# Mask phase of a two-layer cross-attention kernel: row sums scaled at another place, casts and the first turn in a new order

## The reference, cut to what matters

```python
xq = layer_norm(x, qn_w, qn_b)
ctx = layer_norm(context, cn_w, cn_b)
q = xq @ q_w;  k, v = halves of ctx @ kv_w          # 16 heads of 32
attn = einsum('bnhd,bmhd->bhnm', q, k) * scale
attn = where(xa_mask, -max, attn)
attn = softmax(attn, axis=-1)
out = einsum('bhnm,bmhd->bnhd', attn, v) @ proj_w + proj_b
x = x + out
```

## Time and profile before

| What | us |
|---|---|
| median of three runs | 2664.84 (2664.46 to 2666.05) |
| the profiled execution's own time | 2662.04 |
| its span in the profile | 2660.3 |
| busy TensorE | 2592.9 (97%) |
| busy VectorE | 1940.7 (73%) |
| busy ScalarE | 1559.0 (59%) |
| busy GpSimd | 922.3 (35%) |
| mean granted clock of TensorE | 0.995 of full |

### The profile page before, as it was taken

The page is one execution under the profiler, slowest core; times in us unless marked ns, Lnnn a source line. Parts: engine busy times, 40 slices in busy tenths (PEclk is TensorE's granted clock), DMA queues, the critical chain, the costliest instruction groups (busy, mean ns, idle before and its releaser), DMA issues.

```text
span 2660.3 us, 67274 instructions
## 1 busy us (share of the span) xinstructions
PE 2592.9 (97%) x23144; PEld 2230.5 (84%) x23144; DVE 1940.7 (73%) x5443; ACT 1559.0 (59%) x4742; POOL 922.3 (35%) x1098
## 2 busy tenths in 40 slices
PE   6999999998999999999999999999999999999997
PEld 5788888887888888888888888888788888888886
DVE  6888888887534443444378888887788888888877
ACT  6787777876211111111267777777676776767764
POOL 4766676662111001100113333333442434424331
PEclk9999999999999999999999999999999999999999
DMA  5766667674210211022021111112321322212210
GB/s 165 184 165 168 168 170 189 165 189 132 72 59 32 63 47 47 32 63 87 25 96 48 47 47 47 47 47 80 100 80 63 98 68 71 87 63 95 71 48 25
DMA packets 313622, 236.12 MB, mean 89 GB/s; under 512 B 150736, under 2 KB 240848, under 8 KB 312656
## 3 DMA queue, kind: packets, MB, share of 16 engines
q1 hardware_dynamic: 313552, 235.22, 30.9%
HBM read 137.65 MB, written 63.96 MB: 76 GB/s over the span
## 4 chain that ended last, share of the span: by engine, by line
PE 77%; DVE 10%; ACT 7%; issue 4%; POOL 0%; DMA 0%; DVEq 0%; ACTq 0%; POOLq 0%; SPq 0%
PE cross_work L181 17%; PE mlp_acc L3297 13%; PE mlp_f L3279 13%; PE causal_work L181 10%; PE cross_scores L2294 3%; PE mask_work L181 3%; ACT mask_prob_even L965 2%; ACT mask_prob L965 2%; PE cross_scores L2271 2%; PE cross_attended L2324 2%; PE causal_scores L2294 2%; PE causal_scores L2271 2%; DVE mask_scores L1552 2%; PE causal_attended L2324 2%; DVE mask_stats L1465 1%
## 5 line engine op out<-in xcount | busy, mean ns | idle before, releaser
L3072 ACT ACTIVATE mlp_h<-mlp_f,mlp_b1col 128x512 f32<-128x512 f32 x128 | 88.3, 690 | 525.9 <-PE mlp_f L3279 525.9
L3279 PE MATMUL mlp_f<-mlp_xT_hi,mlp_w 128*128 128x512 f32 x1024 | 335.7, 390 | 0.9 <-DVE mlp_xT_lo L3165 0.9
L3179 DVE CAST mlp_hT_hi<-mlp_h 128x512 fp32r<-128x512 f32 x128 | 58.2, 454 | 369.9 <-ACT mlp_h L3072 369.7
L3297 PE MATMUL mlp_acc<-mlp_w,mlp_hT_hi 128*128 128x512 f32 x1024 | 315.5, 389 | 0.0
L965 ACT ACTIVATE cross_prob<-cross_scores,cross_low 128x256 f32<-128x256 f32 x512 | 237.1, 490 | 63.4 <-DVE cross_low L1546 63.4
L965 ACT ACTIVATE causal_prob<-causal_scores,causal_low 128x128 f32<-128x128 f32 (+1 forms) x512 | 210.1, 436 | 93.7 <-DVE causal_low L1552 93.6
L3279 PEld LDWEIGHTS mlp_f<-mlp_xT_hi,mlp_w 128*128 128x128 f32 x1024 | 192.3, 188 | 41.3 <-DVE mlp_xT_lo L3165 1.3
L3297 PEld LDWEIGHTS mlp_acc<-mlp_w,mlp_hT_hi 128*128 128x128 f32 x1024 | 192.3, 188 | 39.8
L181 PE MATMUL causal_work<-causal_xT_hi,causal_w 128*128 128x256 f32 x1008 | 217.1, 294 | 0.3 <-DVE causal_qk_parts L1500 0.3
L1552 DVE CUSTOM_DVE_ANT_0 mask_scores<-mask_scores,mask_mask 128x256 f32<-128x256 f32 x512 | 200.5, 456 | 22.1 <-PE mask_scores L2271 13.6
L736 POOL TENSOR_SCALAR causal_q<-all_own_head,causal_qk_parts 128x128 fp32r<-128x128 f32 x128 | 60.1, 481 | 406.2 <-DVE causal_qk_parts L1500 395.9
(11 more groups left out here) (369 smaller groups left out, 8093.4 us busy)
## 6 DMA issues: line engine op xcount, KB each, us to landing
cross_x_in<-after_attention SPq DMA_DIRECT2D x17, 512.0 KB, 4.1
mask_x_in<-in_x SPq DMA_DIRECT2D x16, 512.0 KB, 4.2
mask_c_in<-in_ctx SPq DMA_DIRECT2D x16, 512.0 KB, 4.8
mask_res<-in_x SPq DMA_DIRECT2D x16, 512.0 KB, 3.7
after_attention<-mask_res SPq DMA_DIRECT2D x16, 512.0 KB, 3.4
mlp_x<-after_attention SPq DMA_DIRECT2D x8, 1024.0 KB, 5.5
mlp_stage<-in_L_xattn_fc_w SPq DMA_DIRECT2D x8, 1024.0 KB, 5.6
after_layer<-mlp_y SPq DMA_DIRECT2D x8, 1024.0 KB, 4.4
```

The costliest lines, as they stand in the source:

```text
L3279: ins = pe.matmul(F1[m % 2][:], W[2 * (m // 4)][:, a, k, m % 4 * P:(m % 4 + 1) * P], xT[p][:, k, :], start=(k == 0 and n == 0), stop=(k == ...
L3297: ins = pe.matmul(ACC[t][:], hT[a][:, m % 2, t * P:(t + 1) * P], W[2 * (m // 4) + 1][:, p, m % 4, :], start=(m == 0 and n == 0), stop=(m = ...
```

## The change

Five moves, with one wait taken away and one added.

1. over_sums of chunks 2 and 3 (reciprocal and copy) moves from the end of a turn to behind minima(b, 0) of the next. `sums` is therefore indexed with p % 2.
2. In middle turns normed(b, 0) moves ahead of front(b + 2).
3. ScalarE casts V (values_high) behind units 4 and 5, and casts both halves of chunk 2 behind unit 11; exps of unit 10, the copy of Q and K for chunk 3, and exps of unit 11 come ahead of them.
4. Turn 0: the casts of the projection matrix go from ScalarE at the end to GpSimd at the start (with a wait for ScalarE's first 12 casts), its remainders on VectorE from the end to behind minima(0, 1). The remainders of x go ahead of the transposes of the context, the Q/K remainder of chunk 3 behind them. GpSimd casts x ahead of the gains of the context, and no longer waits for VectorE ahead of low_halves(0, 2). TensorE turns the sums behind the queries of turn 1.
5. Turn 15: the projection's second half and turn_probs(7) go ahead of the MLP work put in there, and the turn of sums behind projection and scores.

```diff
--- before.py
+++ after.py
@@ -783,6 +783,9 @@
             if masked_ctx:
                 if nxt:
                     normalise(b + 1)
+                    if not prev:
+                        pool.wait_ge(s["w_hi_done"], KC * 3)
+                        matrix_hi(3)
                 elif cur:
                     yield ROOM
                 if prev:
@@ -797,11 +800,18 @@
                 values_low(b)
                 if nxt:
                     gain(b + 1, 1)
+                    if not prev:
+                        turned_hi(b + 1, 0)
+                        turned_hi(b + 1, 1)
                     gain(b + 1, 2)
                     gain(b + 1, 3)
-                    for k in range(NP):
-                        turned_hi(b + 1, k)
-                    pool.wait_ge(s["t_lo"], NP * (b + 2))
+                    if prev:
+                        turned_hi(b + 1, 0)
+                        turned_hi(b + 1, 1)
+                    turned_hi(b + 1, 2)
+                    turned_hi(b + 1, 3)
+                    if prev:
+                        pool.wait_ge(s["t_lo"], NP * (b + 2))
                 low_halves(b, 2)
                 return
             if causal:
@@ -1062,12 +1072,12 @@
             high_halves(b, 0, 0)
             high_halves(b, 0, 1)
             values(b, 1)
-            values_high(b)
             if not nxt:
                 yield ROOM
 
             exps(b, 4)
             exps(b, 5)
+            values_high(b)
             exps(b, 6)
             qk(b, 2)
             exps(b, 7)
@@ -1084,10 +1094,10 @@
 
             exps(b, 8)
             exps(b, 9)
+            exps(b, 10)
+            qk(b, 3)
+            exps(b, 11)
             high_halves(b, 2, 0)
-            exps(b, 10)
-            exps(b, 11)
-            qk(b, 3)
             high_halves(b, 2, 1)
             pair_kept(b, 0)
             if not nxt:
@@ -1099,8 +1109,6 @@
                 qk(b + 1, 0)
             exps(b, 14)
             exps(b, 15)
-            if not prev:
-                matrix_hi(3)
             if nxt and not prev:
                 qk(b + 1, 0)
             copy(b, 12)
@@ -1390,7 +1398,7 @@
             act.sem_inc(common.s["past_cross"], 1)
 
     def vector(dve):
-        head = {"mask": 6, "causal": 9, "cross": 13}[kind]
+        head = {"mask": 5, "causal": 9, "cross": 13}[kind]
         per = {"mask": 4, "causal": 13, "cross": 19}[kind]
         chain = Chain(dve, s["chain"], head, per)
         def matrix_lo(i, quarters=range(KC)):
@@ -1556,7 +1564,7 @@
         def over_sums(b, p):
 
             dve.wait_ge(s["exp_done"], UNITS * b + 2 * HC * (p + 1))
-            chain.done(dve.reciprocal(rs[:], sums[:, p]))
+            chain.done(dve.reciprocal(rs[:], sums[:, p % 2]))
             chain.wait()
             dve.tensor_copy(rs32[:], rs[:].unsqueeze(3).to_broadcast([P, TT, 2 * HC, DH])).then_inc(s["rs_done"], 1)
 
@@ -1693,6 +1701,7 @@
         def mask_turn(b, prev, cur, nxt, after=True):
 
             if not cur:
+                over_sums(b, -1)
                 post_lo(b, 0)
                 normed(b, -1)
                 post_lo(b, 1)
@@ -1711,6 +1721,8 @@
             minima(b, 1)
             if nxt and prev:
                 turn_over(b + 1, 0)
+            if not prev:
+                matrix_lo(3)
             qk_lo(b, 2)
             if nxt and prev:
                 turn_over(b + 1, 1)
@@ -1727,52 +1739,44 @@
                 project(b, 0)
 
             minima(b, 2)
-            if not (nxt and prev):
-                over_sums(b, 0)
-            if not nxt:
-                yield ROOM
-            if not prev or not nxt:
-                qk_lo(b, 3)
-            if not prev:
-                turn_over(b + 1, 2)
             if nxt and prev:
                 for k in range(NP):
                     turned(b + 1, k)
                 qk_lo(b, 3)
                 over_sums(b, 0)
+                project(b, 1)
             elif nxt:
-                turn_over(b + 1, 3)
+                over_sums(b, 0)
                 turned(b + 1, 0)
                 turned(b + 1, 1)
+                turn_over(b + 1, 2)
+                turn_over(b + 1, 3)
+                qk_lo(b, 3)
             else:
-                yield ROOM
-            if nxt and prev:
-                project(b, 1)
+                over_sums(b, 0)
+                yield ROOM
+                qk_lo(b, 3)
+                yield ROOM
 
             minima(b, 3)
             if not nxt:
                 yield ROOM
                 project(b, 1)
-            if nxt and prev:
-                qk_lo(b + 1, 0)
-                mask_floats(b + 1)
-                if after:
-                    front(b + 2)
-            normed(b, 0)
-            if nxt and not prev:
+                normed(b, 0)
+                yield ROOM
+                yield ROOM
+                return
+            if not prev:
+                normed(b, 0)
                 turned(b + 1, 2)
                 turned(b + 1, 3)
-            over_sums(b, 1)
-            if not prev:
-                matrix_lo(3)
-            if nxt and not prev:
-                qk_lo(b + 1, 0)
-                mask_floats(b + 1)
+            qk_lo(b + 1, 0)
+            mask_floats(b + 1)
+            if prev:
+                normed(b, 0)
+            if after:
                 front(b + 2)
-            elif not nxt:
-                yield ROOM
-                yield ROOM
-            if nxt and not after:
+            else:
                 yield ROOM
 
                 dve.sem_inc(s["chain"], 2)
@@ -2483,14 +2487,13 @@
                 pe.wait_ge(s["v_ready"], 2 * b + 2)
                 project(b, 0, 0)
             turn_probs(b, 6)
+            if prev:
+                project(b, 0, 1)
+            turn_probs(b, 7)
+
             if not nxt:
                 scores_taken(b, 7)
                 yield ROOM
-            if prev:
-                project(b, 0, 1)
-            turn_probs(b, 7)
-
-            if not nxt:
                 yield ROOM
             scores(b, 2)
             pe.wait_ge(s["qk_lo"], KC * b + 3)
@@ -2505,14 +2508,13 @@
             if not nxt:
                 scores_taken(b, 11)
                 yield ROOM
-            if not (nxt and prev):
-                turn_sums(b, 0)
 
             if not nxt:
                 yield ROOM
             scores(b, 3)
             if not nxt:
                 project(b, 1, 1)
+                turn_sums(b, 0)
             if nxt and prev:
                 pe.wait_ge(s["qk_lo"], KC * (b + 1))
                 pe.wait_ge(s["t_lo"], NP * (b + 1) + 2)
```

2 lines of the change are left out of this document (1 added, 1 removed).

## The result

The changed kernel takes 2641.39 us, the median of four runs (2640.74 to 2643.01), against 2665.45 (2664.46 to 2666.70) of the kernel before on the same chip: a ratio of 0.991, 95% interval 0.9893 to 0.9928. The profiled execution took 2641.75 us with a span of 2640.0, so the two traces differ by 20.3 us where 15.2 were forecast; the other 3.8 of the 24.1 is the kernel before, whose runs lie 2.4 to 4.7 us above its profiled one. Run once more in a later series, the changed kernel took 2641.54 against 2662.46, 20.9 less.

A forecast was written before the change was run, and what follows sets the result against it. TensorE was taken to set the middle turns, so only its idle time could be won: 14 turns at -0.63 give -8.8, turn 0 -5.5, the end -0.9, sum -15.2 us from 2664.84: 2649.6, range 2642 to 2658.5.

The forecast's parts named there:

- the safety of the transposes: Middle turns, chunk 2: later GpSimd remainders still let the transposing DMA land before TensorE wants it, 0.9 to 1.3 us cover.
- the sum of the ends: Turn 0 plus turn 15 and the end of the mask phase: together -6.4 us.
- second cast order: Middle turns, ScalarE's chunk 2 casts behind unit 11: TensorE's wait ahead of the fourth scores goes, -0.41 us a turn.
- values_high behind units 4 and 5: Middle turns: unit 5 done one cast earlier, so TensorE's wait for it goes, -0.25 us a turn.
- scaling of the first pair first: Middle turns, VectorE: scaling ahead of the statistics removes TensorE's wait before the attended product, -0.17 us a turn.
- reciprocal and copy behind the next minima: Middle turns, VectorE: a new TensorE wait of 0 to 0.4 us ahead of the turn of sums, taken as +0.2.
- Rival E: Middle turns: busy rows may hide small stalls that fall too, 1.2 us a turn, -23.2 in all, 2641.6 us; chance 0.06.
- Turn 0: First turn: moved projection-matrix casts and remainders let turn 1's attended product start at 67.3 us, -5.5 (-8 to -3).
- Turn 15 and the end: Last turn: reciprocal and copy leave the front of the minima, a turn of MLP rows moves; -0.9 us (-2 to +1).
- Rival D: Middle turns, chunk 2: later GpSimd remainders make transposes land after TensorE wants them; slower, 2680.4 us at 8.0 landing; chance 0.04.
- Rival B: Middle turns: VectorE's copy always slow under GpSimd's normalising, TensorE waits 0.4 us for sums; -12.4, 2652.4 us; chance 0.18.
- Rival C: Middle turns: a VectorE and ScalarE ring of 37 us holds the turn, only the ends gain; -6.4, 2658.4 us; chance 0.10.

The follow-up runs named there:

- casts_alone: Kernel before with one move: both ScalarE casts of chunk 2 behind unit 11 and the copy of Q and K; 2651.64 us, ratio 0.9948.
- vh_back: Changed kernel with ScalarE's cast of V (values_high) back ahead of the exponentials of units 4 and 5; 2641.34 us, ratio 0.991 to the kernel before.
- sums_casts: Kernel before with two moves: second reciprocal and copy behind the next first minima, both chunk 2 casts behind unit 11; 2643.57 us, ratio 0.9918.
- t0_split: Changed kernel, VectorE's turn 0 reordered: projection-matrix remainders split two and two, z scaled behind the context's remainders; 2640.29 us, ratio 0.9912 to the kernel before.
- t0_alone: Kernel before with only the change's turn 0 part, the reciprocal and copy staying at the turn's end; 2656.88 us, ratio 0.9971.
- best: t0_split plus, in middle turns, V's second cast behind copies 4 to 6, GpSimd's V remainder behind three gains, VectorE's second transpose earlier; 2634.90 us.
- floats_vh: Changed kernel with values_high back ahead of unit 4 and, in middle turns, VectorE's mask conversion behind the statistics; 2640.65 us, ratio 0.9909 to the kernel before.

## Why the prediction was right and wrong

The direction, the safety of the transposes and the sum of the ends were right; within turn 0 two errors cancel, see below. The step that failed is the middle turn, forecast at -0.63 and measured at -1.11 us. It was mis-sized in each of its four terms:

| Term | forecast | measured |
|---|---|---|
| second cast order | -0.41 | -0.61 (casts_alone) |
| values_high behind units 4 and 5 | -0.25 | -0.15 alone, -0.05 in the change (vh_back) |
| scaling of the first pair first | -0.17 | **+0.28** (vh_back against sums_casts) |
| reciprocal and copy behind the next minima | **+0.2** | **-0.61** alone, -0.32 within the change |

The measured steps add up: -0.61 and -0.61, 0.12 more for the two together, +0.28 and -0.05 make the -1.11.

- **The worst step was the last.** The prediction saw "about 1 us leaves the place ahead of the minima", then followed only the copy to its consumer, the turn of sums, and not the minima to theirs. Behind them lies ScalarE's chain to the third scores, so here the gain was. The feared wait didn't come: the copy ended 0.26 us before TensorE came to the sums.
- **Two waits in one stretch were added up.** The waits for z and for unit 5 both lie in stretch A, whose length ScalarE's chain sets. Removing one lets TensorE run into the chain's end. By the prediction stretch A was to change by -0.25 - 0.17 + 0.2 = -0.22; it changed by -0.50, for another reason.
- **Idle time was taken for the cost of a stall.** The casts' move shortened the turn by 0.61, where the idle column says 0.41. Rival E stood on this mechanism and got 0.06: hidden stalls in busy rows, here 0.61 us a turn. That its 2641.6 is the nearest number is partly luck: it forecast 23.2 us less, and the traces differ by 20.3. The Trainium skill (Perfetto Trace Analysis, Identifying the Most-Contended Engine) says that matmul busy time is not a good measure of how near TensorE is to its limit, and the trace agrees: 36.16 against 35.55 us for the same matmuls. "The rows show no place for it" was wrong: a comparison of the same step with and without its stall, as the turns of probabilities 12 and 13 (from 215.66 to 216.60, 0.94 us) against 4 and 5 (1.32, with 0.25 idle shown), showed it.
- **The scaling of the first pair.** The 0.17 ahead of the attended product is gone, but in sums_casts, without this move, it is gone too (one wait of 0.2 us in 13 turns). And now the statistics stand last, and the minima begin 1.55 us behind the scores (212.63 against 211.08); in sums_casts, with z last, it is 215.27 - 214.08 = 1.19:

```profile
211.97 0.16 DVE L1481 TENSOR_SCALAR mask_rstd<-mask_mv 128x4 f32<-128x4 f32 x1
...
212.63 0.43 DVE L1560 CUSTOM_DVE_ANT_0 mask_scores<-mask_scores,mask_mask 128x256 f32<-128x256 f32 x1 [0.50 <-PE mask_scores L2275]
```

```profile
214.38 0.68 DVE L1567 TENSOR_TENSOR mask_z<-mask_ot,mask_attended 128x512 f32<-128x512 f32 x1
...
215.27 0.43 DVE L1552 CUSTOM_DVE_ANT_0 mask_scores<-mask_scores,mask_mask 128x256 f32<-128x256 f32 x1 [0.21 <-PE mask_scores L2272]
```

  So ScalarE's chain starts later, and the move is the 0.28 us a turn by which sums_casts is shorter than vh_back. Why the minima start that much later behind the statistics is open, see the last section.
- **Turn 0** came out by its own steps. VectorE and GpSimd:

```profile
38.81 3.94 DVE L1407 SCALAR_TENSOR_TENSOR mask_w<-mask_raw,mask_w 128x512 fp32r<-128x512 f32 x4
...
54.38 0.43 DVE L1560 CUSTOM_DVE_ANT_0 mask_scores<-mask_scores,mask_mask 128x256 f32<-128x256 f32 x1 [1.25 <-PE mask_scores L2275]
```

```profile
55.04 4.52 POOL L694 TENSOR_TENSOR mask_prob_parts<-mask_prob_even,mask_prob_parts 128x512 f16<-128x512 f32 x4
```

```profile
60.76 0.39 PE L181 MATMUL mask_work<-mask_cT_hi,mask_w 128*128 128x256 f32 x1 [2.10 <-DVE mask_cT_lo L1496]
...
68.48 0.40 PE L2342 MATMUL mask_attended<-mask_probT_parts,mask_v_part 128*32 128x256 f16 x8
```

  Forecast: 3.6 us, 54.6, 55.3, 60.9 and 67.3. The attended product came 1.2 late. The term that failed is the 5.4 us from the first key product to the end of the turn of probabilities 15: before, that stretch (62.75 to 68.10) ran at a granted clock of 1.00, now its first 5.4 us (60.76 to 66.16) at 0.68, and turn 1's scores started 6.8 us behind the first key product. In return TensorE was at 1.00 from 68 to 78, where before it was at 0.83, so the lead grew from 4.3 us at the attended product to 5.7 at the sums. That the total of turn 0 fits the forecast of 5.5 is thus partly luck. Turn 15 and the end gave 0.4, forecast 0.9.
- **Rival D stayed away, narrowly.** GpSimd ended the remainders of chunk 2 at 242.18 (forecast 252.0 on the old time scale), landings took up to 5.1 us, so by 247.3; TensorE came at 247.86. The forecast cover of 0.9 to 1.3 us was 0.6, since TensorE comes sooner and the longest landing took 5.1, not 4.9. (By the prediction's own sum this rival decides from a landing of 257.8 - 252.0 = 5.8 us on, not from 5.5.)
- **Rival B** did not come: at the copy's new place it took 0.52 us, nearer its shortest 0.43 than its longest 1.30. It was weighed by a rule of the Trainium skill (SBUF — State Buffer, Who interferes with whom), that a copy in a two-port mode and a GpSimd instruction lock each other out for a whole instruction. This place hardly tests the rule, as GpSimd's normalising ended 0.24 us after the copy began (216.48 and 216.24). The copy of the first pair, begun at 237.60, 0.15 us behind GpSimd's remainders, took 1.30 in the same turn.
- **Rival C**, another ring, was right in kind: stretch A was such a ring. It was wrong that nothing in the change reached it.

The miss of 8.2 us is thus 5.1 in the trace (5.4 too little in the middle turns, 0.3 too much at the ends) and 3.2 between profiled executions and medians: the forecast subtracted from a median that lay 2.8 above its profiled execution, and the changed kernel's median lies 0.4 below its own.

## What to carry to other kernels

Price a stall by the starts: the same step with it and without it, not the idle column. Before adding up waits, cut the turn into stretches between two points of the bounding engine and ask of each which other engine runs through it without a pause; within such a stretch only the chain's start and content count, and a cured wait comes back under another name. When a step leaves a queue, follow first what stands behind it to its last consumer, and only then the step itself; when a producer is moved back, look at what is queued behind its consumer.

## What the runs showed of the hardware

- TensorE's granted clock between 58 and 68 us differed from run to run: 0.96 in t0_split, 0.83 in the change, 0.66 in t0_alone and in best, so part of the time it was at 1.2 GHz instead of 2.4. In best it was 1.00 in the 10 us before, in which TensorE was busy for 6.3.
- A row of four pipelined transposes prints 0.60 us, while work whose data is ready starts 0.36 behind the row's start (226.63 and 226.99 in the kernel before). So an idle time shown behind such a row is an estimated 0.24 us less than the stall costs; at units 4 and 5 it was 0.28.
- VectorE's context remainders in turn 0 took 2.33 us for two, with GpSimd's remainders beside them for the first 1.2 us, against 1.28 in the kernel before with GpSimd idle. The Trainium skill (SBUF — State Buffer, Who interferes with whom) says that a VectorE instruction with two inputs in SBUF contends with GpSimd's reads; the trace agrees.
- VectorE's first minima begin 0.36 us later behind two short statistics operations in the loop than behind the 0.68 us of z (1.55 and 1.19 above), and in the turn behind the loop, also behind the statistics, 1.18 (535.18 against scores at 534.00). That the loop's branch is what delays them would explain it, but this is not shown; the one run that tried it (floats_vh) had a wait of its own.
